# Sparse cross attention with seven block products: VectorE's reciprocal of a row's divisors in two halves, placed between other additions

## What is computed

```python
def sparse_norm(scores, nbias):
    t = jax.nn.relu(scores + nbias[0])
    t = t * t
    return t / (t.sum(-1, keepdims=True) + IEPS)      # IEPS = 1e-32
rq = (iQ @ Wq.T).reshape(b, q, H, ADIM)
kv = (iK @ Wkv.T).reshape(b, s, 2, H, ADIM)
rk, rv = (kv[:, :, 0], kv[:, :, 1])
scores = jnp.einsum('bqhd,bshd->bhqs', rq, rk) / sqrt(ADIM)
scores = jnp.where(mask[:, None, :, :], jnp.float32(-1e+32), scores)
attn = sparse_norm(scores, nbias)
o = jnp.einsum('bhqs,bshd->bqhd', attn, rv).reshape(b, q, H * ADIM)
return o @ Wo.T
```

## Time and profile before

| | |
|---|---|
| runs (us) | 3618.01, 3618.47, 3612.85; median 3618.01 |
| profiled execution | 3617.83 us, its span 3616.0 us |
| PE busy | 3381.6 us, 94% of the span |
| VectorE busy | 2184.9 us, 60% |
| ScalarE, POOL busy | 48%, 26% |
| granted TensorE clock, mean | 0.97 of full speed |

### The profile page before, as it was taken

How to read it: one execution, slowest core, us unless ns; L and a number is a source line. 1 busy time by engine, 2 the same in 40 slices (tenths; PEclk the granted TensorE clock), 3 DMA queues, 4 the chain that set the end, 5 groups by cost and what they waited for, 6 DMA issues and landing times. The chain is left out here.

```text
span 3616.0 us, 92938 instructions
## 1 busy us (share of the span) xinstructions
PE 3381.6 (94%) x40208; PEld 2404.2 (66%) x40208; DVE 2184.9 (60%) x4354; ACT 1721.6 (48%) x3173; POOL 934.8 (26%) x584
## 2 busy tenths in 40 slices
PE   7999999989998979999989998999999789999996
PEld 4777777656676668888754455777777565565554
DVE  5666667654444267777645484777777555555337
ACT  4777777623332268887645452444444242112224
POOL 2776777311010000000031122333332003332002
PEclk9999999999999999999998999999999889999998
DMA  2111111021001415344010002111110002220430
GB/s 83 40 39 39 39 57 39 13 92 35 32 1 61 160 38 193 107 160 166 15 53 1 0 1 70 41 55 47 41 61 22 25 12 96 102 97 21 172 132 17
DMA packets 154962, 223.46 MB, mean 62 GB/s; under 512 B 39327, under 2 KB 134235, under 8 KB 154428
## 3 DMA queue, kind: packets, MB, share of 16 engines
q1 hardware_dynamic: 154556, 217.51, 18.0%
HBM read 216.44 MB, written 1.05 MB: 60 GB/s over the span
## 5 line engine op out<-in xcount | busy, mean ns | idle before, releaser
L3622 POOL TENSOR_TENSOR x_sc<-x_sc,h_T 128x2048 f32<-128x2048 f32 (+1 forms) x105 | 443.6, 4262 | 197.8 <-ACT h_T L3849 197.8
L3420 DVE SCALAR_TENSOR_TENSOR x_sc<-ps,x_nb,x_cap 128x2048 f32<-128x2048 f32 (+1 forms) x112 | 246.0, 2196 | 34.9 <-PE ps L3288 34.6
L3924 DVE TENSOR_TENSOR x_most<-x_most,ps 128x512 f32<-128x512 f32 (+1 forms) x352 | 234.8, 685 | 46.5 <-PE ps L3739 34.1
L3350 ACT ACTIVATE x_sc<-x_sc,x_nb 128x2048 f32<-128x2048 f32 (+1 forms) x112 | 210.9, 1883 | 65.1 <-DVE x_sc L3420 65.0
L1795 ACT ACTIVATE s1i_both<-ps,s_less,s_rs_s 128x64 f32<-128x64 f32 x624 | 214.7, 428 | 48.4 <-DVE s_less L1912 48.4
L3828 ACT COPY x_sc<-ps 128x1024 f32<-128x1024 f32 x192 | 179.3, 945 | 110.9 <-PE ps L3739 70.4
L3842 ACT ACTIVATE x_sc<-x_sc 128x2048 f32<-128x2048 f32 (+1 forms) x112 | 200.8, 1797 | 3.7 <-DVE x_sc L3622 3.7
L3695 PE MATMUL ps<-x_wv,x_ctx_T 128*128 128x256 f32 (+1 forms) x832 | 201.4, 384 | 0.0
L3687 PE MATMUL ps<-x_ctx_T,x_wk 128*128 128x401 f32 (+1 forms) x512 | 196.6, 522 | 4.5 <-POOL x_v L3651 3.8
L2062 POOL COPY a_bv_wide<-a_b_col 128x256 f32<-128x256 f32 x2 | 0.8, 396 | 689.4 <-SPq L2058 689.4
L3695 PEld LDWEIGHTS ps<-x_wv,x_ctx_T 128*128 128x128 f32 (+1 forms) x832 | 150.7, 186 | 39.5 <-issue 3.0
(11 more groups left out here) (601 smaller groups left out, 7627.0 us busy)
## 6 DMA issues: line engine op xcount, KB each, us to landing
x_ctx_T<-in_ctx_T SPq DMA_DIRECT2D x32, 1601.0 KB
s1i_ctx_T<-in_ctx_T SPq DMA_DIRECT2D x16, 1601.0 KB, 7.3
x3i_ctx_T<-in_ctx_T SPq DMA_DIRECT2D x16, 1601.0 KB, 7.0
s1i_ctx_n<-in_ctx SPq DMA_DIRECT2D x16, 1536.0 KB
x3i_ctx_n<-in_ctx SPq DMA_DIRECT2D x16, 768.0 KB
h<-in_ctx SPq DMA_DIRECT2D x12, 896.0 KB
e_w<-in_L_attn_W SPq DMA_DIRECT2D x8, 1024.0 KB, 7.1
rows<-in_ctx SPq DMA_DIRECT2D x12, 640.0 KB
```

The lines of the kernel that those rows point to most:

```text
L3350: nc.scalar.activation(x, x, ACT.Square, scale=DH ** -0.5, bias=nb[0:keys, 0:1]).then_inc(squared, 1)
L3420: nc.vector.scalar_tensor_tensor(out=slot[0:keys].rearrange("p r m h j q -> p (r m h) (j q)")[:, :, 0:width], in0=score_banks[0:keys].rear ...
L3622: return eng.tensor_tensor(x, x, most_of, ALU.subtract)
L3924: ins = nc.vector.tensor_tensor(best[0:keys, rs], best[0:keys, rs], score_banks[0:keys, rs, :, j, :], ALU.max)
```

## The change

The reciprocal of a batch row's divisors becomes two instructions over 128 columns each, `invert 0` and `invert 1`, in a function of its own. Both stand in VectorE's list of unit 3: the first between the reading of the divisors and c12 of group 1, the second between c12 and shared of group 2. The two multiplications, the rest of `divide`, move behind c21 in the list of unit 4. `numbered`, which counts the semaphores of the products, leaves the four names out. After the last batch row the reading, both halves and the division follow one another.

```diff
-                 3: [(1, "c22"), (1, "c21"), (1, "den"), (1, "c12"), (2, "shared"),
-                     (2, "three")],
-                 4: [(2, "c22"), (2, "c21"), (2, "values"), (2, "c12")],
+                 3: [(1, "c22"), (1, "c21"), (1, "den"), (1, "invert 0"), (1, "c12"),
+                     (1, "invert 1"), (2, "shared"), (2, "three")],
+                 4: [(2, "c22"), (2, "c21"), (2, "divide"), (2, "values"), (2, "c12")],
...
+    OF_ROW = ("den", "invert 0", "invert 1", "divide")
+
...
-                 if x != "den"]
+                 if x not in OF_ROW]
...
+                def invert(row, half):
+                    cols = slice(2 * half * S, 2 * (half + 1) * S)
+                    dve.wait_ge(den_read, row + 1)
+                    steps.done(nc.vector.reciprocal(rden[:, cols], rden[:, cols]))
+
                 def divide(row):
-                    dve.wait_ge(den_read, row + 1)
-                    steps.done(nc.vector.reciprocal(rden[:, :], rden[:, :]))
                     steps.wait()
...
                     for g, x in DVE_TAKES[u]:
-                        if x != "den":
+                        if x not in OF_ROW:
                             combine(row + 1, g, x)
+                        elif row > 0 and x == "den":
+                            read_denominators(row - 1)
+                        elif row > 0 and x == "divide":
+                            divide(row - 1)
                         elif row > 0:
-                            read_denominators(row - 1)
-                    if u == 3 and row > 0:
-                        divide(row - 1)
+                            invert(row - 1, int(x[-1]))
                 read_denominators(B - 1)
+                for half in range(2):
+                    invert(B - 1, half)
                 divide(B - 1)
```

## The result

| | before | after |
|---|---|---|
| median of 11 runs each (us) | 3618.68 (3612.58 to 3627.13) | 3602.80 (3598.45 to 3608.22) |
| profiled execution, its span (us) | 3617.83, 3616.0 | 3601.77, 3600.0 |
| the stage, first mask to last division (us) | 601.25 | 587.08 |
| a full batch row of it, by the starts of the reading of the divisors, median of 13 (us) | 38.16 | 37.21 |

The changed kernel is faster by 0.44%: the ratio is 0.9956, 95% interval 0.9946 to 0.9967. By the median that is 15.9 us; 3604.0 had been forecast.

What follows compares the result with a forecast made beforehand. PE was taken to bound the sparse cross attention stage, with one stall per row: 14 x 0.96 = 13.44 us and 0.45 in the last batch row, together 13.9, gave 3604.0 us. Range 3598 to 3609, or to 3611 with C.

Steps and rivals of the forecast that it cites:

- The stall and its price: Unit 4, sparse cross attention: PE's "third" of group 2 waits for c22 in 14 batch rows, 0.96 us each.
- The halves: Unit 3: two reciprocals of 0.95 us each hide in VectorE's idle time before c12 and shared.
- c22's slack: Unit 4: c22 done at 2538.39, wanted by PE at 2539.61; 1.2 us of slack in place of the stall.
- One sign of the forecast: VectorE, behind unit 3: mask(4) starts 0.07 us behind its scores, with idle time in front.
- The division: Unit 4, behind c21: two multiplications, 0.41 us, hidden with 0.8 us to spare.
- The last batch row: No products there, so VectorE's chain shows on PE: mask(4) 0.50 us earlier, +0.05 at the very end, net -0.45 us.
- The sum: Whole kernel: 14 x 0.96 = 13.44 us, and 0.45 in the last batch row, together 13.9 us; 3603.9 us.
- A: Unit 3: each half waits for the POOL subtraction under way; gain 0.80 us per row, 3606.2 us; chance 4%.
- B: Unit 3: half 0 waits out POOL's whole run; new stall of 2.0 us per row, 3632 us; chance 2%.
- C: The 766 us behind the stage: clock falls shift, 7.7 us per point of mean clock; about 3610 us; chance 8%.
- D: Unit 4: c22 is late for another reason than the queue, or something else comes late; 3618 us; chance 3%.

Runs made afterwards that it cites:

- e6: The kernel before plus a spare 128x128 reciprocal ahead of the true one at the end of unit 3; ratio 1.0048 to the kernel before, row 38.97 us.
- e1: Changed kernel with the reciprocal whole at the end of unit 3, only the division moved; ratio 0.9964 to the kernel before, row 37.53 us.
- e8: Changed kernel plus a spare 128x256 reciprocal (1.74 us) at the end of unit 3; ratio 0.9971 to the kernel before, row 37.54 us.
- e2: Changed kernel with the division back at the end of unit 3, only the halves moved; ratio 0.9963 to the kernel before, row 37.21 us.
- e4: Changed kernel with the reciprocal whole, ahead of c12 of group 1 in unit 3; ratio 0.9962 to the kernel before, row 37.41 us.
- e3: Changed kernel with the reciprocal whole, behind c12 of group 1 in unit 3; ratio 0.9950 to the kernel before, row 37.21 us.
- e5: Changed kernel with the reciprocal whole, it and the division both behind c21 of unit 4; ratio 0.9963 to the kernel before, row 37.21 us.

## Why the prediction was right, point by point

**The stall and its price.** "Third" waits for c22, c22 for mask(4), and that for the reciprocal: shown by e6 (more queue, more stall, 0.81 for 0.85) and by e1 (less queue, less stall). 0.96 us per row by starts, not the 0.88 that the row lists: the row shrank by 0.95.

**The halves.** 0.948 us in the median for 0.95 forecast. Half 0 fits the hole: c12 starts 0.04 us behind the modelled end of its product (begun at 2523.53, 0.94 us long), as it did before. Half 1 left 0.44 us of idle time ahead of shared, forecast 0.44. c22's slack: done at 2529.84 + 0.56 = 2530.40, wanted at 2531.60, so 1.2 us, forecast 1.2, and e8 says the same. One sign of the forecast did not show: mask(4) starts 0.08 us behind the end of its scores (2526.33 + 1.17), as foretold, but with no idle time in front, since "three" ends in the same moment (2527.03 + 0.56). The forecast's own rows said so: 2535.04 + 0.56 = 2535.60 against a mask at 2535.57.

**The division** is hidden behind c21, and e2 shows that moving it was not needed for the 14 stalls, only worth something in the last batch row.

**The last batch row** was a little mis-sized: -0.45 had been forecast. The way from the start of the reciprocal to PE's next scores was 2838.94 - 2834.34 = 4.60 us, and is now

```profile
2818.38 1.76 DVE L3440 RECIPROCAL x_rden<-x_rden 128x128 f32<-128x128 f32 x2
2820.06 2.25 DVE L3422 SCALAR_TENSOR_TENSOR x_sc<-ps,x_nb,x_cap 128x2048 f32<-128x2048 f32 x1
```
```profile
2822.37 1.17 PE L3290 MATMUL ps<-x_q_bd,x_k_T 32*128 32x128 f32 x32 [2.09 <-DVE x_sc L3422]
```

2822.37 - 2818.38 = 3.99 us: 0.61 less where 0.50 had been forecast, because the mask stands directly behind a reciprocal now and takes 2.25 us instead of 2.35. Another 0.2 us came ahead of it, in the stretch at the lower clock. At the very end the cost was 0.02, not 0.05.

**The sum**: 13.9 us forecast in the stage, 14.2 measured; 2.4 us more came ahead of the stage and 0.55 went behind it, where nothing was changed. That the profiled execution is lower than the 3603.9 of the sum is this, and it is luck: the first mask of the eleven kernels lies within 5.3 us with the same code ahead of it. The range was narrower than its evidence, too: it took the scatter of the runs, 5.6 us, from three of them, and eleven runs of the kernel before lie within 14.6 us (3612.58 to 3627.13).

**The rivals.** A and B (POOL holds the halves back) are out: the halves lie under POOL's subtractions and take what they take elsewhere, and e4's c12 came late by the reciprocal's own length. By the rule of the Trainium skill ("SBUF — State Buffer", "Who interferes with whom") a VectorE instruction with one operand from SBUF, outside the two-port modes, should not meet POOL at the shared ports; the halves agree (0.948 us in the median under POOL's subtractions, 0.95 for this shape in the earlier trace rows). C: the mean clock behind the stage went from 0.94 to 0.93 and the stretch grew by 0.55 us, so that rounded point was far less than the 7.7 us at which I had priced it. Between the profiled e2 (762.4 us at 0.95) and e3 (772.7 at 0.93) it was some 5 us a point, an estimate from rounded clocks: this stretch can move an execution by as much as the change does, whatever the stage does. By my own price C would have stood at 3603.9 + 7.7 = 3611.6, not at 3610. D is out by e1 and e2.

What the prediction left unasked is whether the split was needed: it argued that the two halves fit the two holes, and not that they had to. e3 and e5 answer that they don't; in the full rows moving the whole reciprocal is worth as much.

## What to carry to other kernels

Find the wait of the bounding engine, follow its queue upward to the first thing that could have started earlier, and ask what stands in between that nobody there needs: any place outside that stretch will do, as long as the overhang stays below the next consumer's slack. Work that out for each consumer (here 0.47, 0.45 and 1.2 us) before splitting an instruction, which costs 0.15 us here when the halves stand apart (twice 0.948 for 1.743) and 0.01 when they follow one another (1.76 for 1.75). Where whole runs of one kernel scatter by 0.4% (14.6 us here), compare a repeating stretch of the trace: one that repeats to 0.01 us decides what eleven runs can't.

## What the runs showed of the hardware that I had not expected

PE's clock fell behind a stall of only 1.69 us: in four of thirteen rows of e6, each time with PE busy in nearly all of the time between such stalls. The stalls of 0.88 us of the kernel before did not do that in the 14 rows of its trace, nor did those of 0.26 us in the traces of e1 and e8. Each fall added 1.5 us, twice the 0.81 by which the stall itself had grown. So a stall on TensorE can cost more than its length.

An instruction of VectorE that needs nothing of the one in front starts 0.08 us before that one's recorded end (mask behind reciprocal: 1.66 us after its start, recorded length 1.74). A dependent one starts 0.04 us after the end (1.78). So taking a dependent pair apart is worth 0.12 us beside the work moved.

An instruction directly behind a reciprocal has a shorter record: the mask 2.25 us, for 2.34 behind a multiplication (e2), and an addition 0.49 us (e3, e4), for 0.55 behind another addition. The next instruction follows sooner by as much (c22 2.17 us behind the mask in e1, 2.26 before).
